# The bias of the edgeless rows in the second graph convolution: added by GpSimd to the residual, or put into PSUM by TensorE

## The reference

```python
def gcn_layer(x, src, dst, W, b, n_nodes):
    h = x @ W
    deg = segment_sum(ones, dst) + 1.0
    dis = rsqrt(deg)
    norm = dis[src] * dis[dst]
    agg = segment_sum(h[src] * norm[:, None], dst)
    agg = agg + h * (dis * dis)[:, None]
    return agg + b

y = relu(gcn_layer(x, src, dst, W1, b1, n))
y = gcn_layer(y, src, dst, W2, b2, n)
x = layernorm(x + y)
...
```

## Time and profile before

| | |
|---|---|
| median of 3 runs | 9802.32 us (9798.62 to 9814.49) |
| the profiled execution's own time | 9807.44 us |
| its span, first to last instruction | 9805.7 us |
| pass g2 in it | from 1261 us to 2120 us of the span |
| busy share of the whole span | PE 63%, weight loads 52%, DVE 75%, ACT 58%, POOL 76% |

### The profile page before, as it was taken

One profiled execution on the slowest core, in us unless ns is written; L12 is line 12 of the kernel. 1 busy time (PEld: TensorE's weight loads), 2 busy tenths in 40 slices (PEclk: granted clock), 3 DMA queues, 4 the chain that ended last, 5 costly groups with the idle time before them and its releaser, 6 DMA issues. The chain is left out here.

```text
span 9805.7 us, 131503 instructions
## 1 busy us (share of the span) xinstructions
PE 6177.6 (63%) x32436; PEld 5071.6 (52%) x32436; DVE 7307.2 (75%) x22701; ACT 5719.7 (58%) x14065; POOL 7491.2 (76%) x6901
## 2 busy tenths in 40 slices
PE   7017766668875666777736766884467676654444
PEld 3016655557764666677736665782245453432222
DVE  8349989978887777799978887665568776864444
ACT  0016667778878999899948887331135443432222
POOL 7756678878869888688847776776777777777777
PEclk9569988889995555689868888665568656765555
DMA  3999988863337777444435554663346443432222
GB/s 101 333 300 314 317 282 309 307 217 105 107 90 237 242 241 241 157 158 158 153 98 183 185 180 160 172 176 92 95 136 191 131 119 107 147 104 67 67 67 61
DMA packets 1024294, 1693.84 MB, mean 173 GB/s; under 512 B 301775, under 2 KB 544661, under 8 KB 1023474
## 3 DMA queue, kind: packets, MB, share of 16 engines
q1 hardware_dynamic: 797008, 1380.40, 41.2%
q0 software_dynamic: 166560, 199.56, 9.5%
q10 hardware_dynamic: 59970, 105.49, 3.1%
HBM read 988.10 MB, written 707.84 MB: 173 GB/s over the span
## 5 line engine op out<-in xcount | busy, mean ns | idle before, releaser
L1357 POOL DMA_INDIRECT g_got<-scaled,row_src x2352 | 2227.1, 947 | 788.5 <-issue 664.3
L909 DVE SCALAR_TENSOR_TENSOR g_sums<-g_got,first,g_sums 128x128 f32<-128x128 f32 (+3 forms) x3136 | 871.9, 278 | 1142.2 <-DMA g_got<-scaled,row_src 1132.0
L301 PE MATMUL g_a_p_z<-sb_L_gnn_W,g_a_u_t 128*128 128x128 f32 (+3 forms) x2574 | 577.7, 360 | 562.9 <-ACT g_a_u_t L1190 181.9
L913 DVE SCALAR_TENSOR_TENSOR g_sums<-g_sums,cont,g_got 128x128 f32<-128x128 f32 (+3 forms) x3128 | 880.1, 281 | 0.0
L1190 ACT COPY g_a_u_t<-g_a_p_t 128x512 f32<-128x512 f32 (+3 forms) x495 | 225.1, 455 | 1094.4 <-PE g_a_p_t L1142 644.0
L301 PE MATMUL g_bb_p_z<-sb_L_gnn_W,g_bb_u_t 128*128 128x128 f32 (+2 forms) x4302 | 756.4, 336 | 117.6 <-DVE g_bb_z L1075 58.3
L301 PEld LDWEIGHTS g_a_p_z<-sb_L_gnn_W,g_a_u_t 128*128 128x128 f32 (+1 forms) x2574 | 422.6, 235 | 730.9 <-ACT g_a_u_t L1190 402.6
L301 PEld LDWEIGHTS g_bb_p_z<-sb_L_gnn_W,g_bb_u_t 128*128 128x128 f32 x4302 | 666.1, 234 | 175.2 <-issue 146.2
L1190 ACT COPY g_bb_u_t<-g_bb_p_t 128x1024 f32<-128x1024 f32 (+2 forms) x294 | 233.9, 796 | 846.9 <-PE g_bb_p_t L292 843.8
L1514 POOL DMA_INDIRECT cg_got_src<-x,row_src x392 | 502.8, 1283 | 119.5 <-issue 119.5
L2495 POOL DMA_INDIRECT gb_got<-x,row_src x392 | 412.6, 1053 | 228.3 <-POOLq L179 124.3
(11 more groups left out here) (492 smaller groups left out, 22854.2 us busy)
## 6 DMA issues: line engine op xcount, KB each, us to landing
raw<-gb_u SPq DMA_DIRECT2D x98, 768.0 KB, 3.9
xs<-f_o ACTq DMA_DIRECT2D x97, 516.0 KB
f_x<-in_x ACTq DMA_DIRECT2D x97, 512.0 KB
g_bb_own<-in_x SPq DMA_DIRECT2D x97, 512.0 KB
wide<-g_bb_o SPq DMA_DIRECT2D x97, 512.0 KB
g_bb_own<-wide SPq DMA_DIRECT2D x97, 512.0 KB
g_bb_res<-in_x SPq DMA_DIRECT2D x97, 512.0 KB
x<-g_bb_o SPq DMA_DIRECT2D x97, 512.0 KB
```

Source lines behind the costliest of these rows:

```text
L301: last = nc.tensor.matmul(dst_psum[0:p, q * g * width:(q * g + n) * width], turned_tile[0:n * k, q * P:q * P + p], weight[0:n * k, 0:n * w ...
L909: nc.vector.scalar_tensor_tensor(out=self.firsts, in0=new, scalar=first[:, col], in1=self.firsts, op0=ALU.mult, op1=ALU.add).then_inc(run_ ...
L913: nc.vector.scalar_tensor_tensor(out=self.part(b.s, c), in0=before, scalar=cont[:, col], in1=new, op0=ALU.mult, op1=ALU.add).then_inc(run_ ...
L1357: pool.indirect_dma_start(got[b.s4][:, c * row:(c + 1) * row], None, table, bass.IndirectOffsetOnAxis(ap=index[:, b.n * CH + c:b.n * CH + ...
```

## The change

A node of a normalised pass that has no edges (only bb in g2) gets a tile `ones` of one partition and 128 elements. In `multiply`, before each group of four products into a PSUM bank, one product with a single contracted row writes the bias into all 128 x 512 elements (`start=True`), and the four products of the rows add onto it (`start=False`). `add_bias` of bb is gone from GpSimd's list, that of a stays. `rows` of bb waits for the residual's load in place of `gained`. TensorE waits for `prepared` once at the start of every graph pass, since VectorE fills `ones` there.

```diff
@@ Node.__init__
+                self.bias_product = self.normal and not self.deep and edges is None
+                if self.bias_product:
+                    self.ones = sb(f"{n}_ones", [1, P])
@@ Node.rows
                 if self.normal:
-                    nc.vector.wait_ge(m.gained, b.n + 1)
+                    if self.bias_product:
+                        nc.vector.wait_ge(m.loaded_c[b.s], (b.pair + 1) * DMA)
+                    else:
+                        nc.vector.wait_ge(m.gained, b.n + 1)
@@ Node.multiply
+                if self.bias_product:
+                    for h in range(0, j, 4):
+                        n = min(4, j - h)
+                        nc.tensor.matmul(self.p_z[0:p, h * D:(h + n) * D], self.ones[:, 0:p],
+                                         self.row_bias[0:1, :].unsqueeze(1).to_broadcast([1, n, D]), start=True, stop=False)
+                        for q in range(h, h + n):
+                            last = nc.tensor.matmul(self.p_z[0:p, q * D:(q + 1) * D], self.u_t[b.s][:, q * P:q * P + p],
+                                                    self.weight[:, :], start=False, stop=q == h + n - 1)
+                    last.then_inc(m.multiplied, 1)
+                    return
                 times_weight(self.p_z, self.u_t[b.s], self.weight, p, j, self.k, self.m).then_inc(m.multiplied, 1)
@@ graph_pass, GpSimd
-                                            *(stage for node, lag, every in nodes for stage in node.on(lag, every, (node.add_bias, 2)))])
+                                            *(stage for node, lag, every in nodes if not node.bias_product
+                                              for stage in node.on(lag, every, (node.add_bias, 2)))])
@@ graph_pass, VectorE and TensorE
+                        for node, _, _ in nodes:
+                            if node.bias_product:
+                                nc.vector.memset(node.ones[:, :], 1.0)
...
+                        pe.wait_ge(prepared, 1)
```

## The result

The changed kernel takes 9965.9 us (median of 4 runs, 9954.66 to 9977.74), the kernel before 9802.68 us in the same runs. The ratio is 1.0165, with a 95% interval of 1.0147 to 1.0182: slower by 163 us, where 35 us less were forecast. The time is outside the range.

A forecast was written before the change was run, and what follows sets the result against it. GpSimd was taken to set g2's pace at 8.46 us per iteration; with DMA's 8.00 us the largest next bound, 8.1 us was assumed, saving 35 us over 97 iterations: 9767 us, range 9737 to 9814 us.

The forecast's parts named there:

- What is removed: GpSimd in g2: 98 additions go, 97 of 2.35 us; its iteration falls from 8.46 to about 6.1 us.
- What takes over: g2's next bound per iteration: VectorE 7.77 us, DMA 8.00 us or TensorE 7.6 to 7.9 us.
- the DMA step: DMA engines in g2: 7.44 us busy per iteration at g1's share of 0.93 gives 8.00 us.
- rival 2: DMA engines in g2 bind earlier, at 8.25 us by g1's bytes: 20 us less, 9782 us; chance 0.12.
- VectorE's floor: VectorE in g2 without its 0.69 us wait for GpSimd: 7.77 us per iteration, the floor of the change.
- the sums behind it: Ends of the range before narrowing: 9735 us from VectorE's floor, 9816 us from the upper end of Rival 1.
- What is added: TensorE in g2: two one-row products of 512 columns per iteration, 1.95 us together, kept at 1.1 to 2.02.
- The loop of 7.6 to 7.9 us: TensorE's g2 iteration at full clock: bb's rows, bias and product, turning bb and a, ScalarE's copy, hops.
- The part that scales with the clock: TensorE's loop in g2: 5.7 us of it scale with the granted clock; 8.5 us at 0.88.
- The clock: TensorE's granted clock in g2, 0.88 before: expected near 1.00, from 6.4 records per us against g1's 6.2.
- Rival 1: TensorE in g2: one-row products do not raise the clock; loop 8.4 to 8.6 us, 9797 to 9816 us; chance 0.20.
- Rival 3: TensorE becomes g2's bound between bb's product and a's copy; 9.1 us at clock 0.80, 9864 us; chance 0.10.

The follow-up runs named there:

- e6: The changed kernel with 128 contracted rows in place of one and g2's stores one iteration later; 9744.18 us, 0.9936 of the kernel before.
- e12: The changed kernel with bb's bias left out, neither GpSimd's addition nor TensorE's product, profiled for one execution; 9805.38 us.
- e7: The changed kernel with bb's bias left out and g2's stores one iteration later; 9729.57 us, 0.9917 of the kernel before.
- e2: The changed kernel with 32 contracted rows of 1/32 in place of one row; 9864.12 us, 1.0065 of the kernel before.
- e10: The changed kernel, still one contracted row, with g2's stores one iteration later; 10004.25 us, 1.0201 of the kernel before.

## Why the prediction was wrong

**What is removed: right in size, wrong in what follows.** The addition is gone and GpSimd is no bound. But it does not run ahead into waits for combined blocks, as was forecast: it waits 96 times, 384.7 us in all, for a's residual rows to land. VectorE's new wait for the residual's load was priced at 0; it is 12.2 us in the pass.

**What takes over: the DMA step failed.** The forecast took the share of g1 and worked out 8.00 us. The DMA engines can do 0.94 and 330 GB/s in g2 (e6), which by the same working is 7.9 us, and the iteration is 7.74 us there, so even that was no bound. What holds g2 at 8.39 us (e12) is the loop through SyncE's queue. It was named, in rival 2, as a side remark on a shorter time to land; that rival's 8.25 us comes near it by luck, since it was worked out from bytes, and the loop's own length was never worked out. That alone would have turned the forecast into no change. VectorE's floor of 7.77 us was right: e6 and e7 run at 7.74 and 7.71 us. The stated range, 9737 to 9814 us, is 2 us narrower at each end than the sums behind it, 9735 and 9816 us.

**What is added: the price was right.** Two products, 1.95 us forecast, 2.10 us measured at the full clock. The loop of 7.6 to 7.9 us is 7.90 us in the trace, in part because errors offset each other: it does not run through VectorE's bb rows, taken as 1.37 us, but through a's product on TensorE, 1.09 us, while bias and bb's products take 1728.59 - 1724.41 = 4.18 us in place of 3.97 us. The part that scales with the clock was taken as 5.7 us, and the two timelines give 13.39 - 7.90 = 5.49 us, with 2.41 us fixed.

**The clock: this step failed, and it is the loss.** The prediction counted what the products stream: 52 records' worth in 8.1 us against 36 in 5.85 us in g1, hence a clock near 1.00. A one-row product streams as many columns as a full one and takes no less time, but with it the clock was 0.80, with 32 rows 0.91, with 128 rows 0.97. Rival 1 had seen that one row might not count like 128, but left the clock where it had been, at 0.88, and so kept the time. That misses that the clock can fall below where it was. A likely reason, argued and not tested, is that at 1.2 GHz the same products are spread over 13.39 us, so that a slow iteration has less work of full rows per us than a fast one. Rival 3, with a chance of 0.10, is what happened. Its mechanism and its place hold. Its deciding point of 0.88 was too low: e2 has 0.91 and takes 8.97 us, already slower than before. Its price of 9.1 us at a clock of 0.80 was low against 9.89 us too. Its formula divides by the mean clock, but time at two levels mixes: 0.6 of the time at 7.90 us and 0.4 at 13.39 us give 9.45 us. The rest is that the mean clock over the whole pass was 0.78, and that iterations at the full clock took 8.17 us on average.

The rule of the Trainium skill that stood with rival 1 (TensorE: Matmul & The Clock Gate, Part 4: transposes do not count as busy in the way that products do) pointed to the right question, what counts. No run here tests it for transposes; what the runs show is of products of few rows. The fabric ceiling of 435 GB/s that the Trainium skill gives in DMA: Bandwidth & Descriptors, Specifications, was approached by nothing: the most that g2 showed is 332 GB/s at a share of 0.95 (e7), and VectorE was the bound there.

Shown by the runs: the clock rises with the contracted rows and the time falls with it, from one row to 32 with nothing else changed in TensorE's loop at the full clock; the removed addition has no value while the stores stand where they do; with both bounds removed the pass reaches VectorE's floor. Not shown: by what measure the chip weighs rows, and why e10 exceeds the change.

## What to carry to other kernels

A product with one contracted row costs its full columns in time, 1.05 us for 512 columns in 32 bits here against 0.86 us over 128 rows, and did not keep the clock up. Where TensorE's loop is near the bound, contract over all rows (1/128 against a bias that stands on all partitions gives the same sum) or use a narrower type. When one engine sets the pace, work out the next loop before pricing its relief, the queue that issues loads behind stores among them: two bounds 0.1 us apart hid each other here. And a bound on a busy share taken from another pass says little about a pass whose transfers are issued in a loop.

## What the runs showed of the hardware that was not expected

- TensorE's granted clock depends on how many rows a product contracts, at the same columns, number and place: 0.80, 0.91 and 0.97 with 1, 32 and 128 rows; with the addition kept, 0.73 and 0.96 with 1 and 128 rows of zeros. Zeros count as rows here.
- One row gives a lower clock (0.80) than no such product at all (0.88 before, 0.85 in e12).
- Fewer rows make nothing faster: a product of 512 columns in 32 bits takes 1.05 us to the next group with 1 and with 32 rows and 0.86 us with 128, and the four full products behind it 1.09 us in place of 0.89 us. With 128 rows the next weight load runs ahead of its product, with 1 and 32 it does not; why is not shown.
